# First attention: the copies of the weighted sums move behind the next slot's clamp, the doubts' count moves ahead of the sums

## The reference

```python
Q = (x_text @ Wq).reshape(Bb, Tt, H, DH)                  # H, DH = 4, 32
K = (x_vision @ Wk).reshape(Bb, Gg, H, DH)
scores = jnp.einsum('bthd,bghd->bhtg', Q, K) / np.sqrt(DH).astype(np.float32)
topv, topi = jax.lax.top_k(scores, K_TOP)                 # K_TOP = 32
probs = jax.nn.softmax(topv, axis=-1)
attn = jnp.zeros_like(scores).at[bi, hi, ti, topi].set(probs)
attn_mean = attn.mean(axis=1)                             # over the heads
c_t = jnp.einsum('btg,bgd->btd', attn_mean, V)            # V = x_vision @ Wv
scale_in, shift_in = jnp.split(c_t @ W_film_in + b_film_in, 2, axis=-1)
x = x * (1.0 + mod_gate * scale_in) + mod_gate * shift_in
```

## Time and profile before

| | |
|---|---|
| median of 3 runs | 2861.34 us (2854.84 to 2862.76) |
| the profiled execution, its own time | 2868.78 us |
| its span | 2866.8 us |
| first clamp of the first attention starts | 202.2 us |
| last copy of a quarter of its sums starts | 1238.4 us |
| busy over the span: PE, DVE, ACT, POOL | 2391.9, 2180.8, 2107.9, 1280.6 us |
| busy in one steady batch of 64.86 us: PE, DVE, ACT, POOL | 54.46, 52.74, 57.73, 50.03 us |

### The profile page before, as it was taken

How to read it: one execution, slowest core, us unless ns; L and a number is a source line. 1 busy time by engine, 2 the same in 40 slices (tenths; PEclk the granted TensorE clock), 3 DMA queues, 4 the chain that set the end, 5 groups by cost and what they waited for, 6 DMA issues and landing times. The chain is left out here.

```text
span 2866.8 us, 61230 instructions
## 1 busy us (share of the span) xinstructions
PE 2391.9 (83%) x19829; PEld 1254.5 (44%) x19829; DVE 2180.8 (76%) x7977; ACT 2107.9 (74%) x3547; POOL 1280.6 (45%) x1753
## 2 busy tenths in 40 slices
PE   7958888888888888766878689999999999999538
PEld 5735555555555555544622123333333333333337
DVE  8828887788887888715745699999999999996413
ACT  5749888888989898823412159989999998999325
POOL 1427777777777777722300152232332222200154
PEclk9988988999889988888978779999999999999669
DMA  8820000000000000054251123434444434330222
GB/s 242 263 95 3 22 14 14 16 14 14 14 13 14 17 21 14 7 193 144 41 138 35 46 79 105 97 99 97 108 106 104 105 99 100 94 61 3 60 97 67
DMA packets 163685, 205.77 MB, mean 72 GB/s; under 512 B 78812, under 2 KB 131330, under 8 KB 163350
## 3 DMA queue, kind: packets, MB, share of 16 engines
q1 hardware_dynamic: 152998, 161.80, 22.2%
q0 software_dynamic: 10352, 39.92, 4.0%
HBM read 135.19 MB, written 66.60 MB: 70 GB/s over the span
## 5 line engine op out<-in xcount | busy, mean ns | idle before, releaser
L2170 ACT ACTIVATE pb<-sps 128x512 f32<-128x512 f32 (+1 forms) x1664 | 897.8, 597 | 137.3 <-PE sps L2112 120.6
L2195 DVE TENSOR_REDUCE mx<-wps 128x2 f32<-128x1024 f32 x768 | 886.1, 1219 | 33.1 <-PE wps L2082 24.4
L1076 DVE MAX8 cand<-sc 128x8 f32<-128x46 f32 (+1 forms) x4480 | 602.9, 199 | 137.5 <-issue 77.9
L2127 PE MATMUL ops<-pb,va 128*9 128x256 f32 x6656 | 515.8, 382 | 9.5 <-issue 2.6
L852 PE MATMUL scores<-ctxT,qT 97*128 97x512 f32 (+1 forms) x1024 | 437.2, 576 | 80.5 <-ACT sc L964 69.5
L852 PEld LDWEIGHTS scores<-ctxT,qT 97*128 97x128 f32 x1024 | 206.8, 212 | 318.2 <-issue 218.4
L735 POOL TENSOR_TENSOR prf<-sc,prf 128x1601 f32<-128x1601 f32 x64 | 229.8, 3590 | 126.9 <-ACT prf L971 126.9
L827 PE MATMUL misc<-diag,prs 128*128 128x128 f32 (+1 forms) x1664 | 237.9, 300 | 7.0 <-issue 6.1
L735 POOL TENSOR_TENSOR prs<-sc,prs 128x1601 f32<-128x1601 f32 x64 | 230.6, 3604 | 16.8 <-ACT prs L971 13.8
L827 PEld LDWEIGHTS misc<-diag,prs 128*128 128x128 f32 (+1 forms) x1664 | 217.2, 207 | 17.3 <-issue 13.9
L2127 PEld LDWEIGHTS ops<-pb,va 128*9 128x9 f32 x6656 | 99.6, 89 | 253.3 <-ACT pb L2170 180.4
(11 more groups left out here) (407 smaller groups left out, 4071.0 us busy)
## 6 DMA issues: line engine op xcount, KB each, us to landing
FO<-keys SPq DMA_DIRECT2D x392, 50.0 KB
XX<-keys SPq DMA_DIRECT2D x392, 50.0 KB
ctxn<-in_ctx_dram SPq DMA_DIRECT2D x32, 576.0 KB
keys<-kpb POOLq DMA_DIRECT2D x42, 400.2 KB, 3.5
toep<-kernpad SPq DMA_DIRECT2D x8, 2048.0 KB, 14.9
values<-s_vs SPq DMA_DIRECT2D x16, 832.0 KB, 6.0
XX<-values SPq DMA_DIRECT2D x16, 832.0 KB, 4.5
keysf<-s_kf SPq DMA_DIRECT2D x16, 800.5 KB
```

What stands on the lines that cost most here:

```text
L1076: st.add(v.max(cand[s % 2][:, 8 + n:8 + n + 7 * NP + 1:NP], sc[s % 4][:, c:c + w]))
L2127: ins = t.matmul(ops[VW * i:VW * i + DH1 + 1, 0:S], va[par][0:kn(kt), kt, 4 * g + i, :], pb[(UNITS * g + 2 * kt + i % 2) % 8][0:kn(kt), i ...
L2170: nc.scalar.activation(pb[(UNITS * g + u) % 8][0:rows_, :, :], sps[(UNITS * g + u) % SB][0:rows_, :, :], ACT.Exp).then_inc(p_ready, 1)
L2195: v.tensor_reduce(mx4[:, m // 2, :, 2 * g + m % 2, c], both, AX.X, ALU.max).then_inc(work_read, 1)
```

## The change

In the table the doubts' place "!" moves to the front in the four slots with sums, and in slot 3 ahead of f0' too. The quarters' copies leave their place at the end of ACT's slots 2, 3, 6 and 7. They follow the clamp of the next slot, two at a time. PE takes its order from the same table, and counts the doubts ahead of the sums. DVE, POOL and SP keep their orders.

```diff
-        STEADY = (("!", "w"), ("q0", "!", "q1"), ("t0'", "!", "t1'"), ("f0'", "t2'", "!", "t3'"), ("!", "u1'"),
-                  ("f1'", "!", "c0", "c1", "c2", "c3"), ("t0", "!", "t1"), ("t2", "!", "t3"))
+        STEADY = (("!", "w"), ("q0", "!", "q1"), ("!", "t0'", "t1'"), ("!", "f0'", "t2'", "t3'"), ("!", "u1'"),
+                  ("f1'", "!", "c0", "c1", "c2", "c3"), ("!", "t0", "t1"), ("!", "t2", "t3"))
+        HELD = ("t0'", "t1'", "t2'", "t3'", "t0", "t1", "t2", "t3")
...
+            def held_of(b, s):
+
+                for name in steps_of(b)[s]:
+                    if name in HELD:
+                        sums_out(bank(b, name), int(name[1]), number(b, name))
+
...
                         below_of(b if s else b - 1, (s - 1) % NS, j - 1)
+                        held_of(b if s else b - 1, (s - 1) % NS)
                         side_of((s - 1) % NS, j - 1)
...
                                 doubts_of((s - 1) % NS, j - 1)
+                            continue
+                        if name in HELD:
                             continue
...
             below_of(B - 1, NS - 1, NS * B - 1)
+            held_of(B - 1, NS - 1)
             side_of(NS - 1, NS * B - 1)
```

## The result

The kernel after takes 2816.4 us (median of 6 runs) against 2863.0 before: a ratio of 0.984 (95% interval 0.981 to 0.987), 46.6 us less. The 2863.0 is the median of 6 runs too; the 2861.34 ahead of the prediction is that of 3 of them. The forecast was 2791 us, 70 us less, with a range of 2762 to 2838. The gain comes in slots 2 and 6, where it was forecast; other slots give back more of it than was allowed for, and two thirds of the forecast gain are left.

A forecast was written before the change was run, and what follows sets the result against it. POOL's ring through ACT's clamp was taken to pace the batch. Terms -3.41 + 0.9 - 2.49 + 0.45 = -4.55 us, over 15.5 batches -70.5 us, gave 2791 us from 2861.34; range 2762 to 2838.

The forecast's parts named there:

- What bounds the kernel: First attention: POOL's ring (cut, ACT's clamp, keep) paces the batch; ACT's waits for PE's sums total 69.7 us.
- Slot 2: The clamp ending slot 2 no longer stands behind the copies; POOL's wait falls from 4.19 to 0.78 us: -3.41 us.
- Slot 6: POOL's keep at 763.51 us no longer waits 2.49 us for the clamp; its FiLM work sets the time: -2.49 us.
- Slots 3 and 7: Slot 3: ACT still waits for t1' behind the clamp, +0.9 us; slot 7: POOL stands behind DVE, +0.45 us.
- PE's order up to there keeps its length: Slot 3's working: PE, having had no pause, still ends t1' at 727.6 us, leaving ACT 0.9 us of wait.
- The stall beside the pair sum: Slot 7: a later small POOL step stands behind DVE's pair sum; +0.45 us taken, between 0 and 1.45.
- the wait moves behind the clamp: Rival: ACT waits for t1' as long behind the clamp; only slot 6's 2.0 us remain: 2830 us; chance 0.19.
- the sign named for being wrong: In the profile after, ACT's waits of 2 us and more for sums in slots 3 and 7 would show error.
- The full 5.9 us: Rival: neither cost in slots 3 and 7 appears, 5.9 us a batch saved: 2755 to 2775 us; chance 0.17.
- Slower, by PE's clock: Rival: PE's new pauses in slots 2 and 6 bring more 1.2 GHz stretches; six give 2914 us; chance 0.07.
- The other places: Slots 4 and 0 take the copies of t2, t3 behind the clamp, covered by POOL's 3.6 us keep: no cost.
- Doubts first: Doubts counted right behind the scores; with the copies gone, ACT ends slot 2 at about 724.5 us; no separate size.

The follow-up runs named there:

- The filled kernel: The kernel after, plus 25 idle products a batch on PE (12 ahead of slot 2's scores, 8 slot 5's doubts, 5 slot 6's scores): 2792.2 us, 0.975.

## Why the prediction was right, and where it was off

*What bounds the kernel* held: slot 2 lost its waits for the sums ahead of the clamp in all 13 batches, and slot 6 too; in eight batches a wait of 0.7 to 1.2 us for the scores stands in slot 6 instead. Term by term, with the change of each slot as the mean over the 13 batches (from the starts of the clamps):

| | forecast, us | measured, us |
|---|---|---|
| slot 2 | -3.41 | -3.33 |
| slot 3 | +0.90 | +1.29 |
| slot 6 | -2.49 | -2.77 |
| slot 7 | +0.45 | +1.38 |
| slot 0 | 0 | +0.48 |
| slots 4 and 5 | 0 | -0.47 |
| batch | -4.55 | -3.43 |

*Slot 2*: in the batch shown 9.85 became 6.45, with POOL's wait at the 0.78 us that was taken for it. *Slot 6* is 3.3 us shorter in the first kind of batch, 2.2 in the second, 2.6 in the third.

*Slots 3 and 7* were the terms mis-sized: 2.67 us together for 1.35. Slot 3 grows by 2.86 us in the first kind of batch and by 0.33 in the others; slot 7 by 2.6 in the second kind and by 0.82 in the others. The step that failed is "PE's order up to there keeps its length". From the start of slot 2's scores to the end of t1' PE took 10.20 us in the row before (717.41 to 727.61) and 11.77 in the batch shown (328.61 to 340.38). The two sums took no longer (5.90 us before, with the doubts between them, and 5.87 after); but the scores ahead of them, 4.50 us before, ran at 1.2 GHz from end to end, 5.81 us, and the doubts' products stand behind them. So t1' came 1.57 us later in its slot than I had it. What the runs put in place of the step: the clock is not a constant of the place. The slow stretch lies in slots 2 and 3 in one kind of batch and in slots 6 and 7 in another.

A second term was left out: two copies that move into slots 3 and 7 are longer (0.96 us) than the two that leave them (0.64 us). The filled kernel, where nothing waits for sums, shows this alone: 7.62 us for 7.29 in slot 3, 7.14 for 6.82 in slot 7. The stall beside the pair sum for which the 0.45 stood came in slot 0. There a POOL step took 1.82 us instead of the 0.19 that it takes at 344.82 us, and ACT did not wait for it:

```profile
376.07 1.82 POOL L745 TENSOR_TENSOR rden<-rden,tmask 128x1 f32<-128x1 f32 x1
```

Slot 7's 0.45 was right neither in its reason nor in its size.

Of the rivals, "the wait moves behind the clamp" is what happened in part, and 2816 lies in its stretch of times: the sign named for being wrong, waits of 2 us for sums behind the clamp, came in slot 3 in the first kind and in slot 7 in the second (2.0 to 2.3 us, both quarters together), nine of 13 batches. That the time lies in the range owes as much to the range's width as to the sum; near the forecast's 60.3 us are only the four batches of the third kind. "The full 5.9 us" was had only with the idle products: 64.86 - 59.25 = 5.6. "Slower, by PE's clock" did not come: the clock rose from 0.89 to 0.91. The Trainium skill's rule on pauses, which stood beside that rival, bore on the kernel before already, where the thin places cost it their share (64.86 us, and 61.41 with products in them).

*The other places*: the two copies that slots 4 and 0 took over (0.64 us) were hidden in slot 4 (7.6 to 8.2 us, 8.24 before) and show in slot 0 (7.84, 7.37 before); that was not allowed for. *Doubts first* was costed with the copies; alone it gains nothing.

Left open: why three orders that wait in different places (the whole change, the held copies alone, the second quarter behind the sign pass) come to 61.43, 61.44 and 61.44 us. It is not that the time at 1.2 GHz is the same in all: it is some 13.7 us in every batch of the kernel before, of the held copies alone and of the second quarter behind the sign pass, but some 11.6 in the mean of the kernel after. That the slow stretches take up what an order saves or adds is shown where a step of 0.69 us was added in a batch of the first kind, and argued for the rest. A rival that no run here tests is that a batch with slow stretches keeps step with the changes of the clock, so that only some lengths are steady: without idle products the means that were met are 64.86, 64.84, 61.43, 61.44, 61.44 and 61.52 us, and none between. If so, the size of the gain was not to be had from a sum of waits at all.

## What to carry to other kernels

When an engine's copy waits for PE, put the instruction that the slowest ring needs ahead of that copy; but ask first why PE is late. If the rows show it at 1.2 GHz behind a thin place, idle products in the thin places can be worth as much as a new order: here 25 a batch gave 3.45 us a batch in the old order, the new order gave 3.43, and both together 5.6, less than their sum (as ratios of the whole kernel 0.989, 0.984 and 0.975). After that, look for the engine that has no wait left (here POOL, then ACT) and move its work to where it still waits.

## What the runs showed of the hardware that was not expected

In the kernel before PE had 5.18 us of products in slot 1's 7.14, paused 1.71 us ahead of the next scores, and ran 6.9 us at 1.2 GHz behind that, in each of the 13 batches; in the kernel after with 12 idle products in that pause, and nowhere else, slots 2 and 3 ran at 2.4 GHz. More products on PE made the kernel faster where they filled such a pause (61.43 to 59.25 us a batch) and slower where they did not (63.0). A step of 0.69 us added to one engine's ring cost 0.09 us a batch with the slow stretches in place and 0.69 in the filled kernel.
